# An eight-core selective-scan block: the last chunk's output product started inside the scan, and a look-ahead removed from TensorE's order

## The reference

```python
xn = layernorm(x)
x_and_res = xn @ in_proj_w.T + in_proj_b
x_in = silu(x_and_res[..., :1024]); res = x_and_res[..., 1024:]
ssm = x_in @ x_proj_w.T + x_proj_b            # 16 + 1024 + 1024 columns
delta = clip(softplus(ssm[..., :16] @ dt_proj_w.T + dt_proj_b), 1e-5, 0.1)
# 16 states n for each feature:
h = clip(h * clip(exp(A * dt), 1e-6, 1) + B * dt * x_in, -100, 100)
y = sum_n(h) * C + D * x_in
attn = (y * silu(res)) @ out_proj_w.T + out_proj_b
ffn  = complex product of the two halves of xn with W_real, W_imag (two small tensors unfolded)
out  = x + attn + ffn
```

## Time and profile before

| what | us |
|---|---|
| timed runs, median of 2 | 2251.49 (2248.07 to 2254.91) |
| the profiled execution | 2251.98 |
| its span, slowest core (2) | 2250.4 |
| spans of the 8 cores | 2228.0 to 2250.4 |
| mean granted TensorE clock of the cores | 0.751 to 0.754 of full speed |

### The profile page before, as it was taken

The page is one execution under the profiler, slowest core; times in us unless marked ns, Lnnn a source line. Parts: engine busy times, 40 slices in busy tenths (PEclk is TensorE's granted clock), DMA queues, the critical chain, the costliest instruction groups (busy, mean ns, idle before and its releaser), DMA issues.

```text
span 2250.4 us, 22151 instructions; the slowest of 8 cores (2228.0 to 2250.4 us)
## 1 busy us (share of the span) xinstructions
PE 1243.4 (55%) x5104; PEld 512.0 (23%) x5104; DVE 1619.8 (72%) x1600; ACT 1269.2 (56%) x2001; POOL 609.0 (27%) x570
## 2 busy tenths in 40 slices
PE   1221846255463857285729572867277637855444
PEld 1111312121121313131314131323132213322012
DVE  2332044169995999499949995899689977999980
ACT  0004464566557955695559655965587558745531
POOL 0000041317122261217131713071307131623101
PEclk9999966677585968596859785977588768866557
DMA  5671322630012301140024003310222032202001
GB/s 158 180 185 62 113 68 41 70 61 24 1 66 71 108 19 61 58 127 19 29 85 123 28 10 103 99 52 10 103 90 61 0 112 81 71 1 75 0 10 66
DMA packets 106886, 151.96 MB, mean 68 GB/s; under 512 B 53232, under 2 KB 53240, under 8 KB 106760
## 3 DMA queue, kind: packets, MB, share of 16 engines
q1 hardware_dynamic: 97128, 120.10, 17.8%
q0 software_dynamic: 6176, 19.93, 4.2%
q10 hardware_dynamic: 3456, 10.52, 1.5%
HBM read 124.26 MB, written 26.25 MB: 67 GB/s over the span
## 4 chain that ended last, share of the span: by engine, by line
PE 36%; DVE 22%; ACT 12%; issue 11%; DMA 9%; POOL 7%; SPq 1%; DVEq 0%; ACTq 0%; POOLq 0%
DVE h_buf L845 20%; PE pS L561 6%; PE pM L692 6%; PE pO L595 5%; PE pM L657 5%; DMA xr_t<-x 5%; PE pO L600 4%; PE pO L657 4%; POOL out_tm L477 4%; PE pO L692 3%; ACT da L905 2%; POOL wf L405 1%; PE pT L523 1%; ACT xnf L1008 1%; PE pO L709 1%
## 5 line engine op out<-in xcount | busy, mean ns | idle before, releaser
L845 DVE TENSOR_TENSOR_SCAN h_buf<-da,cr,Bu 128x512 f16<-128x512 f16 x768 | 1071.4, 1454 | 144.3 <-PE pS L561 78.2
L905 ACT ACTIVATE da<-dlt,ac 128x512 f16<-128x512 f16 x1024 | 690.9, 715 | 264.4 <-DVE h_buf L845 263.6
L561 PE MATMUL pS<-h_buf,eye 128*128 128x512 f16 x1024 | 420.6, 473 | 351.3 <-DVE h_buf L845 339.1
L845 DVE TENSOR_TENSOR_SCAN h_buf<-da,Bu 128x512 f16<-128x512 f16 x256 | 332.7, 1356 | 174.2 <-ACT da L905 116.9
L458 POOL TENSOR_TENSOR Bu<-y_s,sres 128x512 f16<-128x512 f32 x64 | 126.5, 1976 | 791.7 <-DVE y_s L824 791.7
L561 PEld LDWEIGHTS pS<-h_buf,eye 128*128 128x128 f16 x1024 | 107.5, 106 | 599.6 <-issue 538.0
L692 PE MATMUL pM<-xin,rx 128*128 128x512 f16 (+1 forms) x832 | 196.7, 381 | 23.3 <-ACT sres L1040 19.0
L477 POOL TENSOR_TENSOR out_tm<-otm,xr_t 128x1024 f32<-128x1024 f16 x32 | 82.9, 2589 | 210.2 <-DMA xr_t<-x 106.8
L657 PE MATMUL pM<-xnf,rin 128*128 128x512 f16 x512 | 134.5, 412 | 3.9 <-ACT sres L1040 2.5
L595 PE MATMUL pO<-Bu,wo 128*128 128x512 f16 x512 | 132.8, 406 | 3.1 <-POOL Bu L458 3.1
L657 PE MATMUL pO<-xnf,rin 128*128 128x512 f16 x512 | 123.0, 385 | 5.5 <-DMA rin<-wt_in 5.5
(11 more groups left out here) (89 smaller groups left out, 1553.5 us busy)
## 6 DMA issues: line engine op xcount, KB each, us to landing
rin<-wt_in SPq DMA_DIRECT2D x128, 256.0 KB, 2.7
rx<-wt_x SPq DMA_DIRECT2D x128, 256.0 KB, 2.6
x_t<-x SPq DMA_DIRECT2D x32, 512.0 KB, 4.7
xr_t<-x POOLq DMA_DIRECT2D x32, 512.0 KB, 5.0
y<-out_tm SPq DMA_DIRECT2D x32, 512.0 KB, 3.6
wt_in<-rin SPq DMA_DIRECT2D x16, 256.0 KB, 2.5
wt_x<-rin SPq DMA_DIRECT2D x16, 224.0 KB, 3.7
x_t<-w_in ACTq DMA_DIRECT2D x4, 512.0 KB, 3.4
```

Source lines behind the costliest of these rows:

```text
L561: TCH(te.matmul(sbank[:, :], eye16[:, :], h_sl(gn), start=(n == 0), stop=(n == NST - 1)))
L845: s_n = VCH(v.tensor_tensor_scan(h_sl(gn), da_r[gn % DAR][:, :], Bu[P][k][:, :], init, op0=ALU.mult, op1=ALU.add))
L905: ACH(sc.activation(da_r[gn % DAR][:, :], dlt[Ps][k][:, :], AF.Exp, scale=c_(a_cols[k], n)))
```

## The change

There are two edits. The first takes the look-ahead out of `pump`, so that the first layer-norm tile of each window is treated as every other step. The second concerns the last chunk. In window 8, behind the output transposes of chunk 6, PE gets the 32 products of `w_ffn` with chunk 7's `xn_f` for blocks m = 0 to 3, in the four banks `pM1`, `pM2`, `pO1`, `pO2`. Then, for each k, the sums up to 16(k+1)+15 are emitted, PE waits for `attn` of block k, and four products of `w_out[k]` go into the same four banks. Behind the last of them stand blocks m = 4 to 7 with all their 16 products. In window 9 the products are skipped (`continue`), and ACT reads blocks 0 to 7 from the four banks in turn. The number of products doesn't change.

```diff
-                off_p = 12 if w >= 2 else 0
-
                 def pump(_cost=None):
                     B = bnd[sk[0]]
-                    look = (bnd[min(off_p + 4, len(bnd) - 1)] - B
-                            if sk[0] == off_p else 0.0)
                     sk[0] += 1
                     while sqi[0] < len(sq):
                         gn = sq[sqi[0]]
-                        if (gn - 3) * SCAN_NS > B + look:
-                            break
-                        if look > 0 and (gn - 6) * SCAN_NS > B + 10.0:
+                        if (gn - 3) * SCAN_NS > B:
                             break
                         emit_sigma(gn)
                         sqi[0] += 1
@@
                         pump()
+                        if cO == nch - 1 and nch >= 2:
+                            continue
                         if m == 0:
                             wt(te, "g", ("attn", cO * 8 + 7))
@@
+                if w == nch and nch >= 2:
+                    cF = nch - 1
+                    PF = cF % 2
+                    fb = [pM1, pM2, pO1, pO2]
+                    for m in range(4):
+                        if m < 2:
+                            wt(te, "a", ("xpev", cF * 17 + 15 + m))
+                        else:
+                            wt(te, "a", ("aoev", (nch - 2) * 8 + 4 + m))
+                        for k in range(DCH):
+                            TCH(te.matmul(fb[m][:, :],
+                                          w_ffn[k][:, m * 128:(m + 1) * 128],
+                                          xn_f[PF][:, k * TC:(k + 1) * TC],
+                                          start=(k == 0), stop=False))
+                    for k in range(DCH):
+                        hi = 16 * (k + 1) + 15
+                        while sqi[0] < len(sq) and sq[sqi[0]] <= hi:
+                            emit_sigma(sq[sqi[0]])
+                            sqi[0] += 1
+                        wt(te, "g", ("attn", cF * 8 + k))
+                        for m in range(4):
+                            TCH(te.matmul(fb[m][:, :],
+                                          w_out[k][:, m * 128:(m + 1) * 128],
+                                          Bu[PF][k][:, :], start=False,
+                                          stop=(k == DCH - 1)))
+                            if k == DCH - 1:
+                                mark(("outmm", cF * 8 + m), TCH)
+                    while sqi[0] < len(sq):
+                        emit_sigma(sq[sqi[0]])
+                        sqi[0] += 1
+                    for m in range(4, 8):
+                        wt(te, "a", ("aoev", cF * 8 + m - 4))
+                        for k in range(DCH):
+                            TCH(te.matmul(fb[m - 4][:, :],
+                                          w_out[k][:, m * 128:(m + 1) * 128],
+                                          Bu[PF][k][:, :], start=(k == 0),
+                                          stop=False))
+                        for k in range(DCH):
+                            TCH(te.matmul(fb[m - 4][:, :],
+                                          w_ffn[k][:, m * 128:(m + 1) * 128],
+                                          xn_f[PF][:, k * TC:(k + 1) * TC],
+                                          start=False, stop=(k == DCH - 1)))
+                        mark(("outmm", cF * 8 + m), TCH)
@@
-                        bank = [pO1, pO2][m % 2]
+                        if cO == nch - 1 and nch >= 2:
+                            bank = [pM1, pM2, pO1, pO2][m % 4]
+                        else:
+                            bank = [pO1, pO2][m % 2]
                         ACH(sc.activation(ao[m][:, :], bank[:, :], AF.Identity,
```

## The result

The changed kernel takes 2261.04 us (median of 25 runs, 2255.98 to 2276.25), the kernel before 2252.92 beside it (24 runs). The ratio is 1.0048 with an interval of 1.0034 to 1.0062: slower by 8 to 14 us, and far inside the 2%. (In some executions the cores of one die run at a lower clock, whatever the kernel; the ratio leaves these out, so it isn't the quotient of the two medians.) The forecast was 2261.6, 9.6 us more than the profiled execution of before. Since the time is a sum of a gain and two losses, the total says little; the question is whether each term is right.

What follows compares the result with a forecast made beforehand. It took the layer-norm stage's chain through POOL, PE and DVE to bound windows with projections, and DVE's scans windows 8 and 9. 2251.98 - 13.0 + 6.5 + 16.8 - 0.7 = 2261.6 us, range 2244 to 2270.

Steps and rivals of the forecast that it cites:

- The end, -13.0: Behind the last `attn`, 68 products take 16.9 us in place of 29.9 for 128: 13.0 us less.
- the slow start: On PE behind the last `attn`, the first sixteen products take 5.62 us, about ten at the lower clock level.
- Window 8, +6.5: In window 8, 36 products ahead of sum 33 take 10.0 us and delay DVE's scan 41: 6.5 us more.
- Rival 2: The stall in window 8 is mostly absorbed because ACT and POOL were late there too: 2255.1 us, chance 0.12.
- Windows 2 to 7, +16.8: Without the look-ahead, scans fall on POOL's layer-norm column instructions: 2.8 us more per window, 16.8 in all.
- no scan lost: In the layer-norm stage of windows 2 to 7, delayed scans are made up; DVE still gets through scan 54.
- tile 3's columns: In windows 2 to 7, POOL's six column instructions at tile 3 take about 3.8 us, not 1.3.
- the old chunk's tile 2: POOL's add of this tile meets a stopped DVE: 2.12 us instead of 2.87, -0.7 in most windows.
- Rival 1: POOL's column instructions dodge the scans, so taking out the look-ahead is worth 0: 2244.8 us, chance 0.21.
- Rival 3: Layer norms of tiles 1, 2 and 3 collide in full in windows 2 to 7: 2303 us, chance 0.03.
- Window 1, -0.7: In window 1 scans stop after 11, so tile 0's columns on POOL end sooner: 0.7 us less in sum.
- Its three parts: In window 1, tile 0's columns end about 2.6 us sooner, tile 1 gives 1.4 back, tile 3 another 0.5.

Runs made afterwards that it cites:

- edit 2 alone: The changed kernel with the look-ahead put back: 2255.46 us, ratio 0.9979 to the kernel before.
- the kernel with four groups: The kernel before with only the last-chunk change, its 32 early products cut into four groups of eight with sums ahead of each: 2246.43 us, ratio 0.9955.
- edit 1 alone: The kernel before with only the look-ahead taken out, the last chunk as before: 2275.69 us, ratio 1.0084.
- the pair with ACT's columns: The kernel before with layer-norm column arithmetic moved from POOL to ACT, without and with the look-ahead taken out: ratios 0.9898 and 0.9879.
- the load ahead: The kernel before with the residual's load for the next token tile issued ahead of the wait for this one: 2207.72 us, ratio 0.9802.

## Why the prediction was right

**The end, -13.0; measured -12.3.** Sixty products fewer, as said. The step that was a little off is the slow start: I took twenty products at 6.5 us (5.62 for sixteen and four at 0.216), and they took 7.1, so some thirteen ran at the lower level and not ten. This was the term that the Trainium skill ("TensorE: Matmul & The Clock Gate", section "What's actually happening") had warned about: the number of slow ones varies. This trace agrees, from core to core even of one execution: core 2 has thirteen, core 4 none. On core 2 it came to 0.6 us, on core 4 the stretch is 2.3 us shorter.

**Window 8, +6.5; measured +6.4, and +6.0 with edit 2 alone.** The block was 9.8 us, the wait on DVE 8.38, and POOL's add moved into the scans behind it. Rival 2 (the stall is absorbed) is out: the kernel with four groups has a window 8 that is 6 us shorter than that of edit 2 alone, and differs from it in PE's order only.

**Windows 2 to 7, +16.8; measured +17.2, with edit 1 alone +16.1.** The mechanism is right in its steps: no scan lost (through 54 ahead of sum 47), tile 3's columns 3.4 to 3.7 us (forecast 3.8), tile 2's 2.0 to 2.6 (forecast 2.2), the old chunk's tile 2 added in 2.12. From window to window the growth is 3.6, 2.7, 2.2, 1.6, 3.0 and 4.0 us on core 2, scattered about the even 2.8 that I took. Rival 1 (the columns dodge the scans) fell with edit 1 alone, and the proof of the cause is the pair with ACT's columns: with them, edit 1 costs nothing. Rival 3 asked for all tiles to collide in full; tile 1 is at 3.1 us for 3.0 before in this window, and tile 2 lost 0.7 to 1.0 us and not 3.2.

**Window 1, -0.7; measured -0.8.** Its three parts came as forecast: tile 0's columns 1.9 us for 4.6, tile 1's 2.7 for 1.2, tile 3's 1.6 for 1.2.

What the prediction didn't know is how far two unchanged stretches scatter from execution to execution, 5 us each here; the sum of terms could be checked only because each could be read by itself. That the forecast, 2261.6, lies within 1 us of the measured median is luck: the interval is 6 us wide, and the four stretches sum to 10.5 us and not 9.6. What was right is the terms.

## What to carry to other kernels

An instruction of 0.2 us on POOL can be worth a scan of DVE's each time it is issued (1.22 us for 0.19 here), so a chain of small POOL instructions on the path wants either a stopped DVE beside it or another engine; a change of order elsewhere decides which of the two it gets. Work that is put ahead as a filler should be cut to less than the slack of the ring behind it: here the same 32 products cost 6 us as one block and nothing as four. And when a change moves the time by half a percent, it pays to look whether it is the difference of terms that can be had apart, since here one edit was a gain as soon as its filler was spread.

## What was not expected of the hardware

The column steps on ACT cost less than a round trip to POOL at any tile: 2.4 us for eight steps, each 0.20 to 0.29 us long and 0.19 to 0.39 apart, where 0.39 apart had been expected of all. POOL's six columns cost anything between 1.2 us (DVE stopped) and 4.9 (window 7 with the load ahead), and every slow one stands beside a scan.
